# Graph attention and a gated graph network over eight batches: the last layer's state update rewritten as n + z(h - n) on VectorE, and the seam between batches reordered

## The reference

```
x: (8, 1024, 128) float32, adj: (8, 1024, 1024) int32, about 0.2% ones

h = relu(layernorm(x))
# graph attention
Wh = h @ W;  e = leaky(Wh a1 [:, None] + Wh a2 [None, :], 0.2)
p  = softmax(where(adj > 0, e, -9e15))
x  = x + elu(p @ Wh)
h0 = relu(layernorm(x))
# gated graph network, three layers
h = h0;  A = (adj != 0)
for i in 0, 1, 2:
    m = h @ weight[i];  aggr = A^T @ m
    r = sigmoid(aggr w_ir + h w_hr + b);  z = sigmoid(aggr w_iz + h w_hz + b)
    n = tanh(aggr w_in + b_in + r * (h w_hn + b_hn))
    h = (1 - z) * n + z * h
out = x + h
```

## Time and profile before

| | |
|---|---|
| time, median of 3 runs | 695.64 us (695.63 to 695.66) |
| the profiled execution | 695.68 us, its span 693.9 us |
| busy: PE / DVE / ACT / POOL | 623.9 / 521.4 / 453.2 / 282.2 us |
| share of the span | 90 / 75 / 65 / 41% |
| TensorE's granted clock | 0.996 of full speed |
| HBM | 67 GB/s over the span |

### The profile page before, as it was taken

How to read it: one execution, slowest core, us unless ns; L and a number is a source line. 1 busy time by engine, 2 the same in 40 slices (tenths; PEclk the granted TensorE clock), 3 DMA queues, 4 the chain that set the end, 5 groups by cost and what they waited for, 6 DMA issues and landing times.

```text
span 693.9 us, 8823 instructions
## 1 busy us (share of the span) xinstructions
PE 623.9 (90%) x2845; PEld 457.0 (66%) x2845; DVE 521.4 (75%) x1218; ACT 453.2 (65%) x777; POOL 282.2 (41%) x295
## 2 busy tenths in 40 slices
PE   2687899989999899988999889997999899998996
PEld 2465677667686676666776666866766677766774
DVE  5766998489876898669985798768986689656544
ACT  2784786558874678557864588756785577554443
POOL 1203544166242561544442662425615434425442
PEclk9999999999999999999999999999999999999999
DMA  6521130122302132022401223021320131001001
GB/s 222 180 92 61 44 139 31 47 77 92 112 10 92 31 122 92 31 62 67 146 32 45 78 92 95 28 91 31 121 92 27 34 94 60 0 1 30 1 1 30
DMA packets 28670, 47.40 MB, mean 68 GB/s; under 512 B 1672, under 2 KB 19408, under 8 KB 28624
## 3 DMA queue, kind: packets, MB, share of 16 engines
q1 hardware_dynamic: 28624, 46.84, 20.3%
HBM read 42.60 MB, written 4.23 MB: 67 GB/s over the span
## 4 chain that ended last, share of the span: by engine, by line
PE 52%; DVE 20%; ACT 11%; POOL 10%; issue 5%; DMA 1%; DVEq 0%; POOLq 0%; ACTq 0%
PE ps_x L931 14%; PE ps_g L969 8%; PE ps_x L912 6%; DVE score L662 4%; POOL rstd L278 3%; DVE away L646 3%; POOL zh L302 3%; DVE hkT L740 2%; ACT score L390 2%; PE ps_r L978 2%; PE ps_r L980 2%; PE ps_r L979 2%; DVE nn L737 2%; PE ps_z L978 2%; PE ps_z L979 2%
## 5 line engine op out<-in xcount | busy, mean ns | idle before, releaser
L969 PE MATMUL ps_g<-edges,h_hi 128*128 128x512 f32 x384 | 157.8, 411 | 11.7 <-DVE h_lo L746 6.6
L969 PE MATMUL ps_g<-edges,h_lo 128*128 128x512 f32 x384 | 151.9, 396 | 0.0
L300 POOL TENSOR_SCALAR tz<-tz 128x512 f32<-128x512 f32 x48 | 37.0, 771 | 253.8 <-ACT tz L431 253.8
L390 ACT ACTIVATE score<-score,nmax 128x1024 f32<-128x1024 f32 x64 | 73.8, 1153 | 43.8 <-DVE nmax L662 42.8
L931 PE MATMUL ps_x<-probT,h_nat 128*128 128x512 f32 x224 | 98.9, 594 | 0.0
L662 DVE CUSTOM_DVE_ANT_0 score<-score,away 128x1024 f32<-128x1024 f32 x64 | 89.0, 1390 | 8.0 <-ACT score L384 7.0
L969 PEld LDWEIGHTS ps_g<-edges,h_hi 128*128 128x128 f32 x384 | 72.8, 189 | 31.2 <-DVE h_lo L746 10.3
L912 PE MATMUL ps_x<-ident,score 128*128 128x128 f32 x512 | 71.6, 282 | 17.4 <-ACT score L390 16.2
L397 ACT ACTIVATE probT<-ps_x 128x512 f32<-128x512 f32 x128 | 71.0, 597 | 17.3 <-PE ps_x L912 17.2
L969 PEld LDWEIGHTS ps_g<-edges,h_lo 128*128 128x128 f32 x384 | 72.9, 190 | 13.6
L912 PEld LDWEIGHTS ps_x<-ident,score 128*128 128x128 f32 x512 | 59.4, 145 | 34.1 <-ACT score L390 25.4
(11 more groups left out here) (133 smaller groups left out, 1314.0 us busy)
## 6 DMA issues: line engine op xcount, KB each, us to landing
adj_in<-in_adj SPq DMA_DIRECT2D x64, 512.0 KB, 3.3
x_nat<-in_x SPq DMA_DIRECT2D x8, 512.0 KB, 4.7
ej<-ej_kept_at SPq DMA_DIRECT2D x8, 512.0 KB, 3.6
out<-nn SPq DMA_DIRECT2D x16, 256.0 KB, 2.3
probT<-in_L_gnn_weight SPq DMA_DIRECT2D x1, 192.0 KB
probT<-in_L_gnn_w_ih SPq DMA_DIRECT2D x1, 192.0 KB
probT<-in_L_gnn_w_hh SPq DMA_DIRECT2D x1, 192.0 KB
ej_kept_at<-ej_row SPq DMA_DIRECT2D x8, 4.0 KB
```

The source lines that it names most:

```text
L300: pool.tensor_scalar(tz[c][:], tz[c][:], 0.5, 0.5, ALU.mult, ALU.add).then_inc(z_done, 1)
L390: act.activation(score[t % U][:], score[t % U][:], ACT.Exp, bias=nmax[:, t:t + 1], scale=-1.0, accum_out=rowsum[:, t:t + 1]).then_inc(exp_ ...
L969: last = pe.matmul(ps_g[c][:], part[:, s, :], edges[par][:, s, cols(c)], start=(s == 0 and part is h_hi), stop=(s == T - 1 and part is h_lo))
```

## The change

In layer 2 of every batch POOL's `z_times_h` is left out. DVE makes the new state in three passes per half: `last_diff` (d = h - n), and `last_h`, which does e = (tz + 1) * d and h' = 0.5 * e + n; with tz = 2z - 1 this is n + z(h - n). The counts of `z_done` and `zh_done` go from six to four per batch.

Around it the orders of the four engines at the seam are changed: DVE's `norm2` of half 1 comes before `n_input(b, 2, 0)`, `away_tile(b+2, 0)` before `att_half(a, 1)`, `scores(b+2, 0)` before the last half's update, and `out_half` of both halves goes into body(b + 1) for all batches but the last; ACT does `r_gate` of half 1 before `n_gate` of half 0 and `h0_half(a, 1)` before `n_gate` of half 1; PE does `h_back` of layer 2 in body(b + 1), each behind one half of the neighbours. In layer 0 `edge_tile(a, 2)` goes behind `new_h(b, 0, 0)`.

```diff
--- before.py
+++ after.py
@@ -147,7 +147,7 @@
         hn_ps, r_ps, z_ps, in_ps = sem("hn_ps"), sem("r_ps"), sem("z_ps"), sem("in_ps")
         hnb_done, tr_done, tz_done, n_done = sem("hnb_done"), sem("tr_done"), sem("tz_done"), sem("n_done")
         rh_done, pre_done, z_done, zh_done = sem("rh_done"), sem("pre_done"), sem("z_done"), sem("zh_done")
-        zn_done, hk_done = sem("zn_done"), sem("hk_done")
+        zn_done, hk_done, mix_done = sem("zn_done"), sem("hk_done"), sem("mix_done")
         hk_ps, hi_done, lo_done, out_done = sem("hk_ps"), sem("hi_done"), sem("lo_done"), sem("out_done")
 
 
@@ -294,9 +294,9 @@
 
             def z_times_h(b, l, c):
 
-                n = b * QS + 2 * l + c + 1
+                n = b * QH + 2 * l + c + 1
                 h = h0T if l == 0 else hkT
-                pool.wait_ge(tz_done, n)
+                pool.wait_ge(tz_done, b * QS + 2 * l + c + 1)
                 pool.tensor_scalar(tz[c][:], tz[c][:], 0.5, 0.5, ALU.mult, ALU.add).then_inc(z_done, 1)
                 pool.wait_ge(z_done, n)
                 pool.tensor_tensor(zh[c][:], tz[c][:], h[:, cols(c)], ALU.mult).then_inc(zh_done, 1)
@@ -333,10 +333,9 @@
                     split_h(b, l + 1, 1)
                 if attend:
                     rstd2_half(b + 1, 0)
-                z_times_h(b, L - 1, 0)
-                z_times_h(b, L - 1, 1)
                 if attend:
                     rstd2_half(b + 1, 1)
+                if attend:
                     split_h(b + 1, 0, 0)
                     split_h(b + 1, 0, 1)
 
@@ -563,14 +562,18 @@
                 r_gate(b, 2, 0)
                 z_gate(b, 2, 0)
                 hnb_half(b, 2, 1)
-                n_gate(b, 2, 0)
+                if not attend:
+                    n_gate(b, 2, 0)
                 r_gate(b, 2, 1)
+                if attend:
+                    n_gate(b, 2, 0)
                 z_gate(b, 2, 1)
+                if attend:
+                    h0_half(a, a_par, 1)
                 n_gate(b, 2, 1)
                 if prepare:
                     leaky_tile(b + 2, par, 0)
                 if attend:
-                    h0_half(a, a_par, 1)
                     h0T_half(a, a_par, 1)
                 if prepare:
                     leaky_tile(b + 2, par, 1)
@@ -730,14 +733,38 @@
                 dve.tensor_tensor(pre[c][:], pre[c][:], ps_in[:], ALU.add).then_inc(pre_done, 1)
 
             def new_h(b, l, c):
+                n_part(b, l, c)
+                h_sum(b, l, c)
+
+            def n_part(b, l, c):
 
                 n = b * QS + 2 * l + c + 1
-                dve.wait_ge(z_done, n)
+                dve.wait_ge(z_done, b * QH + 2 * l + c + 1)
                 dve.wait_ge(n_done, n)
                 dve.scalar_tensor_tensor(nn[c][:], tz[c][:], 1.0, nn[c][:], ALU.subtract, ALU.mult).then_inc(zn_done, 1)
+
+            def h_sum(b, l, c):
+
+                n = b * QS + 2 * l + c + 1
                 dve.wait_ge(zn_done, n)
-                dve.wait_ge(zh_done, n)
+                dve.wait_ge(zh_done, b * QH + 2 * l + c + 1)
                 dve.tensor_tensor(hkT[:, cols(c)], zh[c][:], nn[c][:], ALU.subtract).then_inc(hk_done, 1)
+
+            def last_diff(b, c):
+
+                n = b * QS + 2 * (L - 1) + c + 1
+                dve.wait_ge(n_done, n)
+                dve.tensor_tensor(zh[c][:], hkT[:, cols(c)], nn[c][:], ALU.subtract).then_inc(zn_done, 1)
+
+            def last_h(b, c):
+
+                n = b * QS + 2 * (L - 1) + c + 1
+                dve.wait_ge(zn_done, n)
+                dve.wait_ge(tz_done, n)
+                dve.scalar_tensor_tensor(zh[c][:], tz[c][:], 1.0, zh[c][:], ALU.add, ALU.mult).then_inc(mix_done, 1)
+                dve.wait_ge(mix_done, b * 2 + c + 1)
+                dve.scalar_tensor_tensor(hkT[:, cols(c)], zh[c][:], 0.5, nn[c][:], ALU.mult, ALU.add
+                                         ).then_inc(hk_done, 1)
 
             def lo_half(b, l, c):
 
@@ -779,9 +806,15 @@
             def body(b, par, attend, prepare):
                 a, a_par = b + 1, 1 - par
 
-                if attend:
+                if b == 0:
                     scores(a, 0)
+                else:
+                    out_half(b - 1, a_par, 0)
+                if attend:
                     away_tile(a, a_par, 1)
+                if b > 0:
+                    out_half(b - 1, a_par, 1)
+                if attend:
                     scores(a, 1)
                 if prepare:
                     norm1(b + 2, par)
@@ -794,8 +827,9 @@
                 n_input(b, 0, 0)
                 if attend:
                     edge_tile(a, a_par, 1)
+                new_h(b, 0, 0)
+                if attend:
                     edge_tile(a, a_par, 2)
-                new_h(b, 0, 0)
                 n_input(b, 0, 1)
                 lo_half(b, 0, 0)
                 new_h(b, 0, 1)
@@ -844,23 +878,28 @@
                 g_lo_half(b, 2, 1)
                 if attend:
                     split_h0(a, 0)
-                    att_half(a, a_par, 1)
-                    x1_sum(a, a_par, 1)
-                n_input(b, 2, 0)
-                if attend:
-                    norm2(a, a_par, 1)
-                    new_h(b, 2, 0)
-                    n_input(b, 2, 1)
-                else:
-                    new_h(b, 2, 0)
-                    n_input(b, 2, 1)
-                new_h(b, 2, 1)
-                if attend:
-                    split_h0(a, 1)
-                out_half(b, par, 0)
                 if prepare:
                     away_tile(b + 2, par, 0)
-                out_half(b, par, 1)
+                if attend:
+                    att_half(a, a_par, 1)
+                    x1_half(a, a_par, 1)
+                    n_input(b, 2, 0)
+                    n_input(b, 2, 1)
+                    last_diff(b, 0)
+                    split_h0(a, 1)
+                    last_h(b, 0)
+                else:
+                    n_input(b, 2, 0)
+                    last_diff(b, 0)
+                    last_h(b, 0)
+                    n_input(b, 2, 1)
+                if prepare:
+                    scores(b + 2, 0)
+                last_diff(b, 1)
+                last_h(b, 1)
+                if not attend:
+                    out_half(b, par, 0)
+                    out_half(b, par, 1)
 
             run(dve, first, body)
 
@@ -1072,7 +1111,12 @@
                     neighbours(b, par, l, 1, 1)
 
 
-                late_neighbours(0)
+                neighbours(b, par, 0, 1, 0)
+                if b > 0:
+                    h_back(b - 1, 2, 0)
+                neighbours(b, par, 0, 1, 1)
+                if b > 0:
+                    h_back(b - 1, 2, 1)
                 if attend:
                     probT_tile(a, a_par, 0)
                 gates_h(b, 0, 0)
@@ -1130,13 +1174,13 @@
                 gates_g(b, 2, 0)
                 gates_h(b, 2, 1)
                 gates_g(b, 2, 1)
-                h_back(b, 2, 0)
                 if attend:
                     neighbours(a, a_par, 0, 0, 0)
-                h_back(b, 2, 1)
-                if attend:
                     neighbours(a, a_par, 0, 0, 1)
                     h0T_half(a, a_par, 1)
+                else:
+                    h_back(b, 2, 0)
+                    h_back(b, 2, 1)
 
             run(pe, first, body)
```

More of the change, by code:

```diff
@@ L780, in body @@
                 a, a_par = b + 1, 1 - par
+                if b == 0:
+                    scores(a, 0)
+                else:
+                    out_half(b - 1, a_par, 0)
                 if attend:
-                    scores(a, 0)
                     away_tile(a, a_par, 1)
+                if b > 0:
+                    out_half(b - 1, a_par, 1)
+                if attend:
                     scores(a, 1)
```

## The result

The changed kernel takes 689.77 us (689.71 to 689.95, 4 runs) against 695.65 for the one before, a ratio of 0.9911 with a 95% interval of 0.9899 to 0.9922. It is faster, by 5.9 us; the prediction was 680.4 with a range of 675.5 to 686.5.

The account below looks back on a forecast made before the run. PE was taken to do most of the pacing, with DVE the new limit at the seam; 0.5 + 5 x (1.7 + 0.5) + 3.0 + 1.85 - 1.05 = 15.3 us off 695.68 gave 680.4, range 675.5 to 686.5.

Parts of the forecast that it names:

- five periods: In each of five periods, 1.7 us won at the seam by earlier g_lo and 0.5 by the moved edge tile.
- seam after batch 5: No norm1 stands before g_lo there, so PE limits itself: 3.0 us gained, no separate 0.5.
- seam after batch 6: No scores stand in the way, back 1 ends last, then out_half and the restart: 1.85 us gained.
- the end: In batch 7 the third passes lie on the last chain, less 0.29 given back: 1.05 us lost.
- DVE's timetable: Start times of DVE's passes at the seam after batch 2: g_lo at 319.7 instead of 321.43, 1.7 us gained.
- rival C: At five seams DVE is hardly slowed beside POOL: 1.06 us more gain each, 675.1 us; chance 0.11.
- Rival B: At 7 seams POOL's split blocks DVE whole, 1.91 us, passes of 1.5 to 2: 0.85 less gain each, 686.4; chance 0.17.
- The edge tile's 0.5 us: In layer 0, tile 2 behind new_h runs after z_times_h has ended on POOL: 0.5 us gained per batch.
- the new PE order: At the seam both last-layer h_back go behind neighbour products needing only h_lo; PE without idle at h_back.
- h0_half earlier: At the seam ACT's h0_half of half 1 ends at 308.0 instead of 312.4, starting some 4.4 us earlier.
- PE reaching gates_g before g_lo: At the seam PE is ready at 318.6, DVE's g_lo ends last, and PE idles some 2 us.
- rival E: At the seam hn_of_h waits for late out_half 1: 706.7 us, chance 0.07; its sign: PE still waits for hkT.

Follow-up runs that it names:

- thin_split: The changed kernel with GpSimd's split of the transposed h0 at the seam on 8 of 512 columns, the rest left out: 678.03 us.
- edge_back: The changed kernel with edge tile 2 put back ahead of new_h(b, 0, 0): 689.34 us.

## Why the prediction was wrong

It foresaw 15.3 us of gain and got 5.9. The spans and starts of gates_g in both traces, in the order of its sum (the periods are cut at gates_g of layer 1, the last two seams at gates_g of layer 0):

| term | foreseen | measured |
|---|---|---|
| batch 0, edge tile | 0.5 | -0.1 |
| five periods | 5 x 2.2 | 3.7 |
| seam after batch 5 | 3.0 | 2.1 |
| batch 6, inner | 0 | -0.1 |
| seam after batch 6 | 1.85 | 1.6 |
| the end | -1.05 | -1.26 |

The measured terms give 5.9 us, the spans 6.0. The five periods hold 7.3 of the missing 9.4: 5 x 0.9 at the seam, 5 x 0.5 of the edge tile, and 0.3 that I cannot place.

The row of batch 0 cannot be put down to the edge tile. In the trace after, TensorE's granted clock is 0.50 (1.2 GHz) from 70 to 75 us, after 2.57 us of idle on PE, and gates_g of layer 0 starts at 79.34; in the trace before, the low stretch lies earlier (0.55 from 63.5 to 67 us) and gates_g starts at 78.63.

*The step that failed is DVE's timetable*, in the sentence that gives last_diff 0.98 and last_h 1 no stretch at all, with the scores at 1.71. Up to 304.74 it held within 0.2 us (moved by the 1.45 us that the batch starts earlier). last_diff 0 took 1.77, so split_h0 began 0.44 late; the scores took 1.22, which won 0.5 back; last_h 1's first pass took 1.67, which lost 0.98. The state was done at 314.09 and g_lo came 0.94 later than foreseen, and the seam gained 0.94 us less the 0.14 named under *Missed*, 0.8 instead of 1.7. thin_split shows the cause: without the long splits all these passes are 0.69 and the time is 678.03. An estimate fits: rival C's 675.1, with no slowing of DVE, plus the edge tile's 6 x 0.5 is 678.1; that it fits so closely is in part luck, as the 0.14 per batch is not in it.

*Rival B was the right mechanism*, and the sign named for it, passes of 1.5 to 2 us beside the splits, is what came. I gave it 0.17 and 686.4 us. It allowed 1.91 us of holding per seam, 0.85 more than the forecast. The held passes come to 1.08 + 0.40 + 0.98 = 2.46 us over 0.69 each, the one beside split 0 among them, which B left out; but the scores were not held, where both B and I had counted on it, so that g_lo was 0.94 late, near B's 0.85. The seam was thus priced about right in B, in part by luck. Most of the 3.4 us between its 686.4 and the 689.8 measured is the 0.5 per batch of the edge tile, which B kept. The Trainium skill, page "SBUF — State Buffer", section "Who interferes with whom", says that whoever issues first holds the pair for the whole instruction; the rows here agree: scores 1.22 and POOL 1.66 where the scores began 0.05 us ahead, last_diff 0 and last_h 1 at 1.77 and 1.67 where POOL was first. I had weighed the rule against a single 0.98 and taken the row. Read beside POOL, the trace before says otherwise:

```profile
314.70 1.60 POOL L315 TENSOR_TENSOR hT_lo<-h0T,hT_hi 128x512 fp32r<-128x512 f32 x1
...
332.50 1.06 POOL L312 TENSOR_SCALAR hT_hi<-hkT 128x512 fp32r<-128x512 f32 x1
...
336.35 1.78 POOL L315 TENSOR_TENSOR hT_lo<-hkT,hT_hi 128x512 fp32r<-128x512 f32 x1
```

The pass of 0.98 met the last 0.45 us of a POOL instruction and ended 0.53 after it, like the held passes above. The scores of 1.71 and 2.31 began 0.63 and 1.22 us before POOL's ends (316.30 and 338.13) and ended 1.08 and 1.09 us after them. An estimate from these rows: a held pass ends at POOL's end plus its length alone, less 0.15 us. The 1.71 that I set against rival B was a whole hold too, beside a remainder.

*The edge tile's 0.5 us was wrong in kind.* I read the pair's 2.37 us as two tiles slowed alike, and moved one out of the contention. It is one tile held to 1.78 and one at 0.69, as the two rows of the trace after show, and together they fill what the pair filled before; edge_back shows that the order is free. This was a term without a gain: 0.5 was foreseen per batch and nothing measured.

*Missed:* norm2 ahead of n_input makes pre late for PE's product of half 1: the seam starts with 0.14 us lost per batch (1.45 to 1.30 at the end of batch 2).

*Right:* that the kernel is faster, the new PE order (first h_back free of waits), h0_half earlier by 4.5 us relative to the last product (from 5.20 us behind it to 0.66, where 4.4 was foreseen), away_tile free in DVE's gap, PE reaching gates_g before g_lo, the seam after batch 6 limited by out_half (1.77 us shorter against 1.85; the 1.6 of the table includes the lost 0.14). After batch 5 PE was the limit, as foreseen, but h_back of half 1 was late by the held passes: 1.27 us of idle, and the seam itself is 2.3 us shorter (16.21 to 13.92) instead of 3.0; the table's 2.1 runs from gates_g to gates_g and includes the lost 0.14. The end cost 0.2 more, and that is the clock. PE's last four transposes took 1.11 us in the trace after and 0.66 in the trace before:

```profile
683.32 1.11 PE L951 MATMUL ps_r<-ident,hkT 128*128 128x128 f32 x4 [3.60 <-DVE hkT L766]
```

The granted clock over these 1.11 us was 0.50 (1.2 GHz), after 3.60 us of idle; in the trace before it was 1.00, after 2.96. In edge_back, whose end is the same code, the idle is 3.60 too, the granted clock 0.86 and the transposes 0.67 us long, and the end costs 0.87 us.

*The sign named for rival E came without E.* PE still waited 1.25 us for hkT, but out_half of half 1 ended at 315.89, long before g_lo, so hn_of_h was not what held gates_g.

Not tried: the split of half 0 at another place, and the holds of layer 1 beside away 3 and scores 3, which are the largest left.

## What to carry to other kernels

Before giving VectorE more work beside GpSimd, lay both engines' timetables side by side and let each pass of VectorE that starts inside a GpSimd instruction end only after it; add up the wait, not a mean slowing. Here this held for passes with two SBUF inputs and also for the edge and away tiles, which have one (1.76 to 1.78 us instead of 0.69). Work that is not due (here half 1's split, due on PE some 13 us later) is best placed beside passes that were not held, here those that read PSUM and bn_stats. And a change of arithmetic and a change of order can each lose alone and win together, so price them together, and follow in-order queues through to what stands third or fourth behind the late instruction.

## What the runs showed of the hardware

A GpSimd instruction of 8 columns, 0.20 us alone, was recorded as 0.79 us where VectorE's scores were running (thin_split). So even a tiny instruction on GpSimd waited out a long pass of VectorE. Four GpSimd passes on each seam, all of them off the chain that sets the end by their own length, cost the whole kernel 11.7 us, against the 26.7 us that they take themselves (14 passes of 0.62 and 14 of 1.29 in seven seams).
